# x by tokens: from TensorE transposes to a second load in 32x32 squares, turned on VectorE

## The reference, cut to what matters

```python
xn = group_norm(x, norm_w, norm_b)                       # 8 groups of 32 channels
q, k, v = split(einsum('oc,bchw->bohw', qkv_w, xn) + qkv_b)
attn = softmax(einsum('bci,bcj->bij', q, k) / sqrt(C))
x = x + einsum('oc,bchw->bohw', proj_w, einsum('bij,bcj->bci', attn, v)) + proj_b
t = to_tokens(x)                                         # (16, 1024, 256)
u = ln(t); n = u / norm(u)
t = t + softmax((n @ n.T) ** 2) @ u
y = ln(t) @ (sign(w - mean(w)) * mean(abs(w))) + bias
t = t + round(clip(y, -1, 1) * 7) / 7
```

## Time and profile before

| engine | busy us | share of the span |
|---|---|---|
| PE | 1840.7 | 98% |
| PEld | 1700.7 | 90% |
| DVE | 1268.5 | 67% |
| POOL | 958.9 | 51% |
| ACT | 906.0 | 48% |

### The profile page before, as it was taken

The page is one execution under the profiler, slowest core; times in us unless marked ns, Lnnn a source line. Parts: engine busy times, 40 slices in busy tenths (PEclk is TensorE's granted clock), DMA queues, the critical chain, the costliest instruction groups (busy, mean ns, idle before and its releaser), DMA issues.

```text
span 1880.5 us, 36857 instructions
## 1 busy us (share of the span) xinstructions
PE 1840.7 (98%) x12834; PEld 1700.7 (90%) x12834; DVE 1268.5 (67%) x2516; ACT 906.0 (48%) x1444; POOL 958.9 (51%) x2262
## 2 busy tenths in 40 slices
PE   8999999999999999999999999999999999999997
PEld 7998999989899998999989999999998999989997
DVE  5676766667666676666767667676676766667566
ACT  3544536345463544635446354454544536355452
POOL 0654727447273472734637256372654727447272
PEclk9999999999999999999999999999999999999999
DMA  2000010000100001000010100001000010000000
GB/s 76 1 24 23 1 45 0 22 22 0 45 0 22 22 0 45 0 33 11 0 45 0 45 0 7 38 0 45 0 22 22 0 45 0 22 22 0 23 1 23
DMA packets 16416, 35.43 MB, mean 19 GB/s; under 512 B 2688, under 2 KB 4096, under 8 KB 16384
## 3 DMA queue, kind: packets, MB, share of 16 engines
q1 hardware_dynamic: 16384, 35.01, 5.1%
HBM read 18.23 MB, written 16.78 MB: 19 GB/s over the span
## 4 chain that ended last, share of the span: by engine, by line
PE 92%; DVE 5%; issue 2%; DMA 0%; ACT 0%; SPq 0%; POOL 0%; ACTq 0%; DVEq 0%; POOLq 0%
PE wide L322 33%; PE narrow L424 7%; PE narrow L426 7%; PE narrow L425 7%; PE turn L434 6%; PE wide L424 5%; PE wide L426 5%; PE wide L425 5%; PE narrow L322 5%; PE wide L520 3%; PE turn L481 2%; DVE prob L930 2%; PE turn L377 1%; PE narrow L452 1%; PE turn L511 1%
## 5 line engine op out<-in xcount | busy, mean ns | idle before, releaser
L322 PE MATMUL wide<-xn_hi,prob 128*128 128x512 f32 x1024 | 310.0, 404 | 0.0
L676 ACT ACTIVATE prob<-turn 128x1024 fp32r<-128x1024 f32 x128 | 131.3, 1026 | 322.1 <-PE turn L434 322.1
L1107 POOL TENSOR_TENSOR ln_v<-ln_mv,ln_eps 128x1 f32<-128x1 f32 x256 | 49.3, 193 | 455.8 <-DVE ln_mv L909 253.7
L690 ACT ACTIVATE ln<-tok,ln_shift,ln_r 128x256 f32<-128x256 f32 x128 | 77.0, 602 | 344.2 <-POOL ln_shift L1112 344.2
L891 DVE TENSOR_REDUCE neg_max<-wide 128x1 f32<-128x1024 f32 x128 | 156.4, 1222 | 122.9 <-PE wide L322 122.9
L424 PE MATMUL narrow<-prob 128*128 128x256 f32 x768 | 225.0, 293 | 0.0
L426 PE MATMUL narrow<-prob 128*128 128x256 f32 x768 | 217.0, 283 | 0.0
L425 PE MATMUL narrow<-prob 128*128 128x256 f32 x768 | 216.9, 282 | 0.0
L322 PEld LDWEIGHTS wide<-xn_hi,prob 128*128 128x128 f32 x1024 | 182.8, 188 | 35.4
L896 DVE TENSOR_TENSOR prob<-turn,prob 128x1024 fp32r<-128x1024 f32 x128 | 156.7, 1224 | 61.8 <-ACT prob L676 61.8
L669 ACT ACTIVATE expo<-wide,neg_max 128x1024 f32<-128x1024 f32 x128 | 142.6, 1114 | 58.2 <-DVE neg_max L891 58.0
(11 more groups left out here) (171 smaller groups left out, 5480.5 us busy)
## 6 DMA issues: line engine op xcount, KB each, us to landing
x_raw<-in_x SPq DMA_DIRECT2D x32, 512.0 KB, 4.0
out<-y_sb SPq DMA_DIRECT2D x32, 512.0 KB, 2.8
tok<-in_L_conv_qkv_w SPq DMA_DIRECT2D x1, 768.0 KB, 6.3
ln<-in_L_conv_proj_w SPq DMA_DIRECT2D x1, 256.0 KB, 6.8
ln<-in_L_ffn_weight SPq DMA_DIRECT2D x1, 256.0 KB, 4.3
out_bias<-in_L_conv_proj_b SPq DMA_DIRECT2D x1, 128.0 KB, 4.1
qkv_b_c<-in_L_conv_qkv_b SPq DMA_DIRECT2D x1, 3.0 KB, 6.6
norm_w_c<-in_L_conv_norm_w SPq DMA_DIRECT2D x1, 1.0 KB, 6.2
```

The lines of the kernel that those rows point to most:

```text
L322: mm = pe.matmul(o, lhsT, r, start=first and i == 0, stop=last and i == len(parts) - 1)
L676: act.activation(eT_hi[:, n % 2], turn[:, :], ACT.Copy).then_inc(eT_hi_made, 1)
L690: act.activation(ln2[:, n], tok[:, n], ACT.Identity, bias=ln2_shift[:, n:n + 1], scale=ln2_r[:, n:n + 1]).then_inc(ln2_made, 1)
```

## The change

PE's two groups of transposes of x and the semaphore `xT_up` go. SP loads every image a second time, into `x_quad`: 32 DMAs of 32 partitions by 8 runs by 32 values (128 bytes), so that each 32x32 square of the tile has its channels in the partitions and 32 tokens along the row. POOL adds the bias of the channel to it (`bias_quads`: one carrier operation and eight additions of one value per partition, behind n = 4 of its loop, for the next image), and DVE turns the squares into `x_tok` with two 32x32 transposes of 128x1024, in step s = 1. The bias is itself turned once at the start. The squares of the next image are loaded when DVE has turned those of the current one; the plain load of x no longer waits for PE. On PE the wait for the last transposed probabilities moves from the first group of x's transposes to the LayerNorm transposes.

```diff
--- before.py
+++ after.py
@@ -54,10 +55,11 @@
     NP = len(PARTS)
-    assert KC == 2 and N == 2 * BANK and C // GROUPS == 32
+    assert KC == 2 and N == 2 * BANK and C // GROUPS == 32 and W == Q
     scale = float(C) ** -0.5
...
     x_d = x.rearrange("b (k p) h w -> b p k (h w)", p=P)
+    xq_d = x.rearrange("b (cb cc) (n tq) w -> b tq cc cb n w", cc=Q, tq=P // Q)
     out_d = out.rearrange("b (k p) h w -> b p k (h w)", p=P)
+        quad_bias = sb("quad_bias", [P, C // Q, Q])
+        x_quad = sb("x_quad", [P, C // Q, NT, Q])
+        QUADS = (P // Q) * (C // Q)
@@ -279,6 +286,11 @@
                     sp.dma_start(x_raw[:, k], x_d[b, :, k]).then_inc(x_loaded[k], 16)
+
+            def load_quads(b):
+                for tq in range(P // Q):
+                    for cb in range(C // Q):
+                        sp.dma_start(x_quad[tq * Q:(tq + 1) * Q, cb], xq_d[b, tq, :, cb]).then_inc(quad_loaded, 16)
@@ -295,15 +307,21 @@
                              ).then_inc(ffn_loaded, 16)
+            load_quads(0)
             def reload(b):
-                sp.wait_ge(xT_up, 2 * b)
                 sp.wait_ge(xn_made, 2 * b)
...
+            def reload_quads(b):
+                sp.wait_ge(xT_made, 2 * b)
+                load_quads(b)
+
             reload(1)
+            reload_quads(1)
             with sp.Fori(1, B - 1) as b:
                 reload(b + 1)
+                reload_quads(b + 1)
                 store(b - 1, 0)
@@ -368,15 +386,6 @@
                           ).then_inc(gn_var_up, 1)
-
-            def x_by_tokens(b, g):
-                if g:
-                    pe.wait_ge(xT_made, 2 * b + 1)
-                for t in range(HT):
-                    for k in range(KC):
-                        mm = pe.transpose(turn[:, t * C + k * P:t * C + (k + 1) * P],
-                                          x_raw[:, k, tile(HT * g + t)], ident[:, :])
-                mm.then_inc(xT_up, 1)
@@ -535,19 +544,15 @@
                 if f is not None:
-                    pe.wait_ge(pT_made, (NT - 1) * f + NT - 1)
-                x_by_tokens(b, 0)
-                if f is not None:
                     pe.wait_ge(t2_made, NT * f + NT - 1)
                 queries(b, 0)
-                x_by_tokens(b, 1)
                 if f is not None:
...
                 if f is not None:
-                    pe.wait_ge(xT_made, 2 * b + 2)
+                    pe.wait_ge(pT_made, (NT - 1) * f + NT - 1)
                     turn_ln2(f, 0)
@@ -572,8 +577,6 @@
                     pe.wait_ge(out_made, 2 * f + 2)
-                else:
-                    pe.wait_ge(xT_made, 2 * b + 2)
                 turn_e1(b, 0)
@@ -871,10 +874,10 @@
             def x_tokens(b, g):
-                dve.wait_ge(xT_up, 2 * b + g + 1)
-                dve.tensor_tensor(x_tok[:, HT * g:HT * (g + 1), :],
-                                  turn[:, :].rearrange("p (t c) -> p t c", t=HT),
-                                  out_bias[:, :].unsqueeze(1).broadcast_to([P, HT, C]), ALU.add).then_inc(xT_made, 1)
+                dve.wait_ge(quad_biased, b + 1)
+                dve.transpose(x_tok[:, HT * g:HT * (g + 1), :].rearrange("p n (cb cc) -> p n cb cc", cc=Q),
+                              x_quad[:, :, HT * g:HT * (g + 1), :].rearrange("p cb n tt -> p n cb tt")
+                              ).then_inc(xT_made, 1)
@@ -972,10 +975,9 @@
                     dve.wait_ge(prep_dve, 9)
-                x_tokens(b, 0)
-                if f is None:
+                    dve.transpose(quad_bias[:, :, :], out_bias[:, :].rearrange("p (cb cc) -> p cb cc", cc=Q)
+                                  ).then_inc(quad_bias_made, 1)
                     signs()
-                x_tokens(b, 1)
                 query_lo(b, 0)
@@ -1012,6 +1014,9 @@
                         gn_sums(b + 1, 1)
+                    if s == 1:
+                        for g in range(2):
+                            x_tokens(b, g)
                 residual1(b, NT - 1)
@@ -1097,6 +1102,13 @@
+            def bias_quads(b):
+                pool.wait_ge(quad_loaded, 16 * QUADS * (b + 1))
+                pool.tensor_mul(carrier_p[:, 2:3], ones[:, 0:1], ones[:, 0:1])
+                for cb in range(C // Q):
+                    last = pool.tensor_scalar(x_quad[:, cb], x_quad[:, cb], quad_bias[:, cb, 0:1], None, ALU.add)
+                last.then_inc(quad_biased, 1)
+
             def norm_lo(b, k):
@@ -1176,6 +1188,8 @@
                         gn_coefficients(b + 1)
+                    if more and n == 4:
+                        bias_quads(b + 1)
                 pool.wait_ge(pv1_up, NT * b + NT)
@@ -1197,6 +1211,8 @@
             gn_coefficients(0)
+            pool.wait_ge(quad_bias_made, 1)
+            bias_quads(0)
             front(0, None, True)
```

More of the change, by code:

```diff
@@ L36 @@
 BANK = 512
+Q = 32
 GROUPS = 8
@@ L153, in build @@
         carrier = sb("carrier", [P, 1])
-        carrier_p = sb("carrier_p", [P, 2])
+        carrier_p = sb("carrier_p", [P, 3])
         inv_sum2 = sb("inv_sum2", [P, NT])
@@ L194, in build @@
         xn_lo_made = sem("xn_lo_made")
-        xT_up = sem("xT_up")
+        quad_loaded = sem("quad_loaded")
+        quad_bias_made = sem("quad_bias_made")
+        quad_biased = sem("quad_biased")
         xT_made = sem("xT_made")
```

## The result

The changed kernel takes 2029.18 us (median of 4 runs, 2025.93 to 2030.53) against 1880.21 (1879.66 to 1881.03) for the kernel before on the same chip: a ratio of 1.079, 95% interval 1.0775 to 1.0805. It is slower, as forecast, but by 149 us instead of 20, and outside the range. The profiled span is 2023.9 us, and one image takes about 126 us instead of 115.54.

The account below looks back on a forecast made before the run. PE, busy for 98% of the span, was taken to bound the kernel. The sum was 1880.5 - 27.8 + 6.4 + 40.6 = 1899.7, forecast as 1900 us; range 1858 to 1945, the forecast's own 1881 to 1930.

Parts of the forecast that it names:

- Removed from PE: Two groups of eight transposes per image, 0.87 us each on the chain, go from PE: -27.8 us net.
- Added on DVE: Two transposes in step s=1, 1.13 us each, delay the first residual and PE's second attention product: 0.40 per image, +6.4.
- the cover: Time from the first residual's multiply-add done on DVE to PE's second attention product beginning: 1.99 us.
- Added on POOL: Carrier and eight additions behind n=4, 0.355 us each, 2.98 in all, make POOL 2.71 late: +40.6 over 15 images.
- its high end (5.0): POOL's additions priced at a two-input 128x256 operation (0.61): 5.0 us, 4.7 late per image, 71 over 15 images.
- Does POOL make this up?: No: lateness of 2.71 reaches PE in full, 1.95 at tile 7's unit rows, 0.76 at DVE's hold behind POOL.
- its wait ahead of the seven transposes: Sign on PE late in the image: the 1.32 us wait for DVE grows to about 2.
- Added transfers: SP's 32 loads of 32 KB per image, about 0.5 us an issue, hidden in a 32 us window: cost nothing.
- the squares were not late: Rival: at 1.13 us an issue the loads overrun the window by 7, POOL waits, 105 more: 2005; chance 0.15.
- the transpose not two passes: Rival: each DVE transpose takes two passes, 3.0 us lost per image instead of 0.4, 42 more: 1942; chance 0.09.

Follow-up runs that it names:

- run 11: Changed kernel with additions at the head of POOL's front, DVE transposes apart in the linear layer, 39 more idle instructions ahead of PE's loop: 1852.86 us, ratio 0.9852.
- run 5: Changed kernel with additions at the head of POOL's front and 72 more idle instructions at the start of PE's program: 1860.83 us, ratio 0.9893.
- run 7: Changed kernel as it is, additions behind n = 4, with 72 more idle instructions at the start of PE's program: 1968.98 us, ratio 1.0470.
- run 12: Changed kernel with all eight additions behind n = 4 in two-operation form, and 40 idle instructions ahead of PE's loop: 1916.00 us, ratio 1.0187.
- runs 5 to 8: Idle instructions added ahead of PE's loop in three versions of the changed kernel, then the kernel before: 1860.83, 1857.24, 1968.98, 1913.27 us.
- run 8: Kernel before, without the change, with 151 more idle instructions at the start of PE's program: 1913.27 us, ratio 1.0169.
- run 3: Changed kernel with the additions moved from behind n = 4 to the head of POOL's front: 1926.12 us, ratio 1.0240.

## Why the prediction was wrong, step by step

| term, us | forecast | measured |
|---|---|---|
| PE's transposes gone, per image | -1.74 | -1.77 (run 11) |
| DVE transposes, per image | +0.40 | +0.35 (run 5 less run 11) |
| additions on POOL, per image of 15 | +2.71 | +7.1 (run 7 less run 5) |
| PE's loop fetched again, per turn of 13 | not there | +4.5 (the change less run 7) |

- *Removed from PE* was right, with what it uncovered: nothing.
- *Added on DVE* was right: 1.20 us a transpose, the residual late by what was left of the cover.
- *Added on POOL* failed at its first line, the price, and its high end (5.0) did not hold the 7.27 either. I had priced a one-operation form by a two-operation row. 15 x (7.1 - 2.71) = 66 us of the miss.
- *Does POOL make this up?* was right in its result, 1:1, and wrong in the place. I let PE wait at tile 7's unit rows; with 7.1 us it waits two tiles earlier, through ACT's queue, which I had not followed. At 3.6 us late (run 12) it is the same: PE waits 0.7 at tile 7, and as much at tile 5, and its wait ahead of the seven transposes stays at 1.3 instead of growing to about 2. The full price is settled later, at DVE's subtraction behind POOL: run 7 has the same 1.3 us wait of PE there, with POOL 7.1 later and the period 7.1 longer. Counted from tile 4's transposes, PE in run 7 is 4.5 later than in run 5 at tile 5, 6.7 at tile 7 and 7.1 at the seven transposes. I read this as POOL setting the end, so that PE's slower clock behind the 4.3 us gap costs nothing of its own in run 7; that was not tried apart.
- *Added transfers* was right in that they are hidden, though an issue takes 0.76 instead of 0.5: 24.4 of a window of 32, no wait.
- *What no step had*: PE's loop. I treated a removal of instructions as safe for PE, and did not ask what stands in the program where. It adds 125.8 - 121.3 = 4.5 a turn, 59 us in 13: two gaps at the loop's head, and the clock behind them. In the changed kernel POOL's lateness and these gaps lie one behind the other, so both are paid.

66 + 59 = 125, against 124 us between the forecast and the profiled span of 2023.9; the smaller terms and roundings make up the difference. Of the rivals none was this: the squares were not late, the transpose not two passes. That the change loses at all comes from both parts: without the second fetch it loses 89 us, and with the additions out of POOL's late stretch, but the fetch, 46; with neither it gains 20 (run 5), or 28 with the transposes apart (run 11).

That the loop's place decides is shown by runs 5 to 8. The reading that it is held as long as it touches few enough blocks fits the starts tried, given against the kernel before: 0, +6 and +39 held, -33 and +151 fetched again. With blocks of 256 and their edges put where they fit, the three touch seven blocks and the two eight; but that place of the edges is chosen to fit, and the exact boundary was not looked for.

## What to carry to other kernels

An edit that adds or removes instructions on PE ahead of a long loop also moves the loop in its program: look at the packets of the instruction queue on the page before and after, and if they rise with the turns, shift the loop by some idle instructions before anything else is judged. Price an operation by a row of the same form, down to the number of its operations, and on an engine that runs back to back behind it put it where that engine idles: here the same eight additions cost 107 us behind n = 4 and nothing at the head of the loop. A wait that the page puts down to an engine is proven only when that engine's work is changed and the wait moves.

## What the runs showed of the hardware that was not expected

- PE's loop of 1655 to 1687 instructions is either kept (19 or 20 packets in a whole run) or fetched anew with nine packets of 16 KB a turn (in run 8 in 12 of 13 turns); in run 3 this costs 5.4 us a turn against run 5, gaps of 2.6 and 1.8 us and a slow clock behind them.
- On GpSimd a TENSOR_SCALAR with one operation on 128x256 takes 0.85 us and with two 0.41; a per-partition operand adds 0.07 to 0.08; a broadcast two-input addition takes 0.62.
- An idle wait is not free on PE: 72 of these instructions moved its first product from 7.4 to 10.6 us, 39 not at all.
- Transfers of 32 KB in runs of 128 bytes are issued at 0.76 us each and land in 2.2; 1 MB of them takes 24.4 us, and in run 11 they cost the period nothing.
